# A routed FFN whose expert pairs add the shared rows and scatter the finished rows into the output

## The chip, the cores and the metric

The kernel runs on one core of one Trainium2 chip. The metric is the device time of one execution in microseconds (us). The kernel before has a median of 659.03 us over three runs (658.07 to 661.3).

## The reference

Four sequences of 1024 tokens with 128 features go through an attention-like recurrence and then through a mixture-of-experts FFN. Only these parts matter here:

```python
# attention: of the 3*N outputs (two of each three zero) the last N are kept
z = jnp.zeros_like(o)
out = jnp.stack([z, z, o], axis=2).reshape(B, 3 * N, H, HD)[:, -N:]
...
x = x + attention(layernorm(x))
# FFN on layernorm(x): one expert of 16 for each token, and a shared FFN for all
_, top_idx = jax.lax.top_k(logits, 1)
scores = jax.nn.sigmoid(logits) * mask
masked_inputs = scores.T[:, :, None] * x[None, :, :]
gate_up = jnp.einsum('eth,ehf->etf', masked_inputs, gate_up_proj)
gate, up = jnp.split(gate_up, 2, axis=-1)
expert_out = jnp.einsum('etf,efh->eth', up * jax.nn.silu(gate), down_proj)
shared = jax.nn.silu(x @ w_gate.T) * (x @ w_up.T) @ w_down.T
out = x + shared + expert_out.sum(axis=0)
```

Since only every third attention output row is not zero, only every third token (1368 in all, "mixed") depends on the recurrence. The other 2728 ("others") can go through the FFN early.

## The kernel before

Token rows lie in the SBUF tile `xf` as 33 rows of 128 features in each of 128 partitions: row `3*s` (eleven of them) holds mixed tokens, the remaining 22 hold others. Some places at the sequences' ends hold no token.

The routed part of either set runs as follows. A routing step on VectorE gives every row a slot in a table in memory in which the rows of one expert lie in whole tiles of 128 (`idx`). POOL scatters the normed and scaled rows by indirect DMA, one tile of 128 rows each, into `xs_others` or `xs_mixed` (`scatter`, line 1010). Two tiles make a pair. For each pair, SP loads the rows (`load`, line 510), TensorE transposes them (line 1895), multiplies by the expert's gate and up weights (line 1901), transposes the hidden rows (1908) and multiplies by the down weights (1918). ScalarE applies silu (887) and copies between PSUM and SBUF (881 for the rows, 891 for the hidden, 896 for the output in `copy_y`), VectorE multiplies gate by up (1345). SP stores the pair's output `e_y` into `ys_...` (line 517). Rows, silu results and outputs are double-buffered by the pair's parity. The order of each engine's work in a pair is written out by hand: TensorE does the first gate projection of pair k+1, the hidden transposes of k, the second gate projection of k+1, the row transposes of k+2, the down projection of k. `over_pairs` runs the pairs in a hardware loop, two per turn, with the last three or four written out behind it.

Others have 38 tiles: twelve pairs run beside the recurrence's chain, seven within its forward steps. Mixed rows have 26 tiles, thirteen pairs (`RUNS[2]`), which run alone at the end of the kernel. Before them stand, in this order, the end of the attention, the norm and the routing of the mixed rows, their scatter (line 1010, eleven DMAs on POOL) beside the shared FFN of the mixed rows (lines 1837, 1838, 846, 1331, 1847; line 1336 adds it to `xf`), and VectorE's add of the others' expert rows to `xf` (line 1618), after which `s_fin` reaches 1.

After the last pair, POOL waits for all stores and gathers the outputs back by slot into `early` (line 1026, eleven DMAs). VectorE adds them to `xf` in two halves (line 1629). SP, once `s_fin` is 1, issues the stores of the other rows to `out` (lines 663 to 667), then those of the mixed rows of each half (line 672); ScalarE issues the rows at the sequences' ends (990, 991). All waits stand in program order on their engine's queue: SP's stores of the other rows stand behind all thirteen pairs. The tables are filled with zeros early on (lines 595, 597), so that unused slots hold zeros. TensorE has two clock levels, and the profile shows the granted share (1.00 or 0.50).

Of the kernel before, what the change touches and what calls it, by code (L numbers as in the profile page):

```python
# [6 lines left out]
F32 = mybir.dt.float32  # L7
# [58 lines left out]

def constants():
# [13 lines left out]
    for t in (OTHERS, MIXED):  # L81
        v = valid[:, t.rows]
        parts["valid_" + t.name] = v
        spare = np.where(v, 0, t.tiles * P + np.cumsum(~v.ravel()).reshape(v.shape) - 1)
        parts["spare_" + t.name] = spare
        assert (~v).sum() <= P
    parts["prefer"] = np.tile(E - np.arange(E)[None, :], (P, 1))
# [100 lines left out]
def build(nc, a, out, xs, ys, scr):  # L188

    ctx = ExitStack()  # L190
    with ctx:
# [7 lines left out]
        normed = nc.dram_tensor("normed", (B, N, D), F32).ap()  # L199

# [4 lines left out]
        eps = sb("eps", [P, 1])  # L205
        warm = sb("warm", [P, 3])
# [107 lines left out]
        for t in (MIXED, OTHERS):  # L314
# [12 lines left out]
            else:  # L327
                rows, scaled = take(t.n * D), take(t.n * D)
                q["rows"] = q["shared"] = [rows[:, j * D:(j + 1) * D] for j in range(t.n)]
                q["scaled"] = [scaled[:, j * D:(j + 1) * D] for j in range(t.n)]  # L330
                q["back"] = rows
# [23 lines left out]
        def xT_shared(t, g):  # L355
# [9 lines left out]
        assert 4 * U * P <= left.shape[1]  # L365
        e_in, e_xT = (left[:, k * 2 * U * P:(k + 1) * 2 * U * P].rearrange("p (b u d) -> p b u d", b=2, u=U)
                      for k in (0, 1))
# [40 lines left out]
        s_gat, s_fin, s_out = {t: two("s_gathered_" + t) for t in fb}, sem("s_final"), sem("s_out")  # L408
        s_ends = sem("s_out_ends")
# [3 lines left out]
        PARTS = ((0, MIXED.n // 2 + 1), (MIXED.n // 2 + 1, MIXED.n))  # L413
# [55 lines left out]
        def over_pairs(engine, run, pair):  # L469
# [3 lines left out]
            looped = (n - 3) // 2 * 2  # L473
            with engine.Fori(0, looped // 2) as half:
                i = half * 2
                for k in (0, 1):
                    pair(i, k, 3)
# [17 lines left out]

        def middle_rows(b):

            n = 3 * SKIP
            return out[b, ROWS - n:(C - 1) * ROWS - n:3, :].rearrange("(g r) d -> g r d", r=L2)
# [25 lines left out]
        def _(sp):  # L525
# [68 lines left out]
            for t in SETS:  # L594
                sp.dma_start(xs[t.name].rearrange("(m p) d -> p m d", p=P),
                             zeros[:, 0:D].unsqueeze(1).to_broadcast([P, t.tiles + 1, D])).then_inc(s_xz, 16)
                sp.dma_start(ys[t.name][t.tiles * P:, :], zeros[:, 0:D]).then_inc(s_xz, 16)
# [63 lines left out]
            for b in range(B):  # L661
                g0 = b * C
                sp.dma_start(out[b:b + 1, 1:ROWS - n, :], xf[g0:g0 + 1, n + 1:, :]).then_inc(s_out, 16)
                for q in (1, 2):
                    sp.dma_start(out[b, ROWS - n + q:(C - 1) * ROWS - n:3, :].rearrange("(g r) d -> g r d", r=L2),
                                 xf[g0 + 1:g0 + C - 1, q::3, :]).then_inc(s_out, 16)
                    sp.dma_start(out[b:b + 1, N - last + q:N:3, :],
                                 xf[g0 + C - 1:g0 + C, q:last:3, :]).then_inc(s_out, 16)
            for part, (lo, hi) in enumerate(PARTS):
                sp.wait_ge(s_fin, 2 + part)  # L670
                for b in range(B):
                    sp.dma_start(middle_rows(b)[:, lo:hi, :], xf[b * C + 1:b * C + C - 1, 3 * lo:3 * hi - 2:3, :]
                                 ).then_inc(s_out, 16)
            sp.wait_ge(s_out, 16 * 7 * B)
            sp.wait_ge(s_ends, 16 * 2 * B)
        @block.scalar
        def _(act):
# [220 lines left out]
            def pairs(run):  # L898
                def pair(i, k, ahead):
# [7 lines left out]
                    copy_y(run, i, k, k % 2, i * 8 + 16 * (k // 2 + 1 + run.base[k % 2]))  # L907
# [77 lines left out]
            n = 3 * SKIP  # L985
            last = N - ((C - 1) * ROWS - n)
            act.wait_ge(s_fin, 3)
            for b in range(B):
                g0 = b * C
                act.dma_start(out[b:b + 1, 0:1, :], xf[g0:g0 + 1, n:n + 1, :]).then_inc(s_ends, 16)  # L990
                act.dma_start(out[b:b + 1, N - last:N:3, :], xf[g0 + C - 1:g0 + C, 0:last:3, :]).then_inc(s_ends, 16)
# [6 lines left out]
        def _(pool):  # L998
            G.memset(zeros[:], 0.0).then_inc(s_zero, 1)
            G.memset(eps[:], LN_EPS).then_inc(s_zero, 1)  # L1000
            G.memset(xf[:], 0.0).then_inc(s_xfz, 1)
            pool.wait_ge(s_wa, 128)
# [4 lines left out]
            def scatter_tile(t, j):  # L1007
                q = fb[t.name]
                pool.wait_ge(s_sc, TB[t.name] + j + 1)
                G.indirect_dma_start(xs[t.name], bass.IndirectOffsetOnAxis(ap=q["idx"][:, j:j + 1].bitcast(U32), axis=0),  # L1010
                                     q["scaled"][j], None).then_inc(s_scat[t.name], 16)
# [8 lines left out]
            def gather(t, pairs):  # L1020
# [4 lines left out]
                for j in range(t.n):  # L1025
                    G.indirect_dma_start(q["back"][:, j * D:(j + 1) * D], None, ys[t.name],  # L1026
                                         bass.IndirectOffsetOnAxis(ap=q["idx"][:, j:j + 1].bitcast(U32), axis=0)
                                         ).then_inc(s_gat[t.name][int(t is MIXED and j >= PARTS[1][0])], 16)
# [130 lines left out]
            pool.wait_ge(s_fa, GA[MIXED.name] + len(MIXED.groups))  # L1159
            m = RUNS[2].n  # L1160
# [905 lines left out]
```

## Time and profile before

| what | us |
|---|---|
| median of three runs | 659.03 |
| profiled execution | 659.8 |
| its span, first to last instruction | 657.7 |
| TensorE matmul busy | 518.7 (79%) |
| VectorE busy | 488.9 (74%) |
| POOL busy | 363.0 (55%) |
| ScalarE busy | 255.3 (39%) |
| mean granted TensorE clock | 0.934 |

The profiled execution took 2.1 us more than its span. Busy shares are averages over stages with different limits. The chain of work that ended last is made of 35% TensorE, 28% VectorE, 14% issue time, 12% POOL and 5% DMA; the mixed pairs and what follows them are its last 81 us. In the rows, "start us, us" are the start and the duration, and "issue" is time in which an engine waited for nothing that the profile shows.

### The profile page before, as it was taken

The page shows a single profiled execution, that of the slowest core. Times are in us where ns is not written, and L with a number is a line of the kernel's source. Part 1 is how long each engine was busy: PE and PEld are TensorE (multiplying, and loading weights), DVE is VectorE, ACT ScalarE, POOL GpSimd, SP SyncE. Part 2 cuts the span into 40 slices and gives each one's busy share as a digit, 9 for nine tenths or more (in the row PEclk, how much of TensorE's full clock was granted, in tenths as well). Part 3 has the DMA queues.
Part 4 walks back from the last instruction along what each step waited for, and adds up shares of the span by engine and source line. Part 5 has one row for each costly group of instructions (what it writes and reads, how often), then busy time and mean ns, then how long its engine had stood idle before and what let it go on. Part 6 is the DMA issues. An engine that isn't in the chain of part 4 may idle for free.

```text
span 657.7 us, 7388 instructions
## 1 busy us (share of the span) xinstructions
PE 518.7 (79%) x1809; PEld 268.9 (41%) x1810; DVE 488.9 (74%) x787; ACT 255.3 (39%) x538; POOL 363.0 (55%) x352
## 2 busy tenths in 40 slices
PE   1778989999999888766878689889999967488930
PEld 0434444445454434222355355434553254245520
DVE  3559999989898999899899998588999766312201
ACT  1815744344535342111433245525545014044510
POOL 4335767666667675565688344476667575600033
PEclk9968999999999998899999799999999977889985
DMA  9601115900000484000431123100100021122134
GB/s 224 140 0 32 33 40 131 258 0 1 0 1 0 119 283 142 1 0 0 118 95 37 40 77 99 49 16 24 32 16 17 5 53 36 43 61 64 56 83 113
DMA packets 46754, 41.79 MB, mean 64 GB/s; under 512 B 4636, under 2 KB 40296, under 8 KB 46216
## 3 DMA queue, kind: packets, MB, share of 16 engines
q1 hardware_dynamic: 43140, 35.61, 19.8%
q0 software_dynamic: 2448, 5.38, 2.9%
q10 hardware_dynamic: 1136, 0.46, 0.3%
q8 instruction: 12, 0.20, 0.1%
q14 instruction: 18, 0.15, 0.1%
HBM read 23.80 MB, written 17.63 MB: 63 GB/s over the span
## 4 chain that ended last, share of the span: by engine, by line
PE 35%; DVE 28%; issue 14%; POOL 12%; DMA 5%; ACT 2%; ACTq 1%; POOLq 0%; DVEq 0%; SPq 0%
DVE grown L1447 9%; PE ps L1901 9%; PE ps L1918 5%; DVE ps L1486 4%; POOL grown L1079 4%; PE ps L1858 4%; PE ps L1908 2%; DVE early L1551 2%; PE ps L1859 2%; DVE grown L1474 2%; PE ps L1958 2%; POOL uv L995 2%; POOL early L1026 2%; PE ps L1663 2%; PE ps L1959 2%
## 5 line engine op out<-in xcount | busy, mean ns | idle before, releaser
L1079 POOL TENSOR_TENSOR grown<-grown 128x512 f32<-128x512 f32 x64 | 80.5, 1266 | 101.0 <-DVE grown L1474 100.8
L1447 DVE TENSOR_TENSOR grown<-ps,steps 128x1536 f32<-128x1536 f32 x64 | 112.1, 1752 | 1.8
L1858 PE MATMUL ps<-grown,cst 128*128 128x512 f32 x128 | 76.3, 680 | 29.4 <-DVE grown L1447 29.3
L870 ACT ACTIVATE uv<-ps 128x512 f32<-128x512 f32 x64 | 38.1, 597 | 109.3 <-DVE grown L1474 109.3
L1901 PE MATMUL ps<-steps 128*128 x128 | 68.7, 635 | 8.5 <-issue 8.5
L1859 PE MATMUL ps<-grown,cst 128*128 128x512 f32 x128 | 69.7, 628 | 0.0
L995 POOL TENSOR_TENSOR uv<-uv,steps 128x512 f32<-128x512 f32 x64 | 67.5, 1075 | 1.6 <-ACT uv L870 1.6
L1345 DVE TENSOR_TENSOR e_h<-rk,ps 128x256 f32<-128x256 f32 x64 | 25.4, 417 | 53.1 <-ACT rk L887 34.3
L1866 PE MATMUL ps<-uv,cst 128*128 128x512 f32 x128 | 60.4, 594 | 0.6 <-POOL uv L995 0.6
L1152 POOL TENSOR_TENSOR early<-state,qT 128x512 f32 x22 | 37.2, 1689 | 34.0 <-DVE state L1461 34.0
L1474 DVE TENSOR_TENSOR grown<-ps,steps 128x512 f32<-128x512 f32 x64 | 43.3, 677 | 8.7 <-PE ps L1858 8.5
L1858 PEld LDWEIGHTS ps<-grown,cst 128*128 128x128 f32 x128 | 22.1, 204 | 63.2 <-DVE grown L1447 57.2
L1486 DVE TENSOR_TENSOR ps<-ps,grown 128x512 f32<-128x512 f32 x60 | 41.6, 693 | 8.3 <-POOL grown L1079 8.3
L1026 POOL DMA_INDIRECT early<-ys_mixed,slots_mixed x11 | 10.6, 964 | 64.5 <-DMA ys_mixed<-e_y 61.5
L1480 DVE TENSOR_TENSOR ps<-ps,steps 128x512 f32<-128x512 f32 x64 | 44.1, 689 | 1.8 <-PE ps L1859 1.8
L1123 POOL COPY early<-early 128x32 f32<-128x32 f32 x63 | 27.3, 435 | 27.9 <-DVE early L1556 27.8
L1551 DVE TENSOR_TENSOR early<-early 128x256 f32<-128x256 f32 x63 | 40.2, 638 | 1.3
L1859 PEld LDWEIGHTS ps<-grown,cst 128*128 128x128 f32 x128 | 26.2, 205 | 34.5 <-issue 34.5
L887 ACT ACTIVATE rk<-ps 128x256 f32<-128x256 f32 x64 | 23.9, 383 | 40.1 <-PE ps L1901 38.4
L1918 PE MATMUL ps<-steps,e_hT 128*128 x256 | 35.8, 283 | 2.7 <-ACT e_hT L891 2.7
L1866 PEld LDWEIGHTS ps<-uv,cst 128*128 128x128 f32 x128 | 24.2, 190 | 31.8 <-issue 29.7
L1918 PEld LDWEIGHTS ps<-steps,e_hT 128*128 128x128 f32 x256 | 31.5, 191 | 8.9 <-issue 8.0
(223 smaller groups left out, 998.5 us busy)
## 6 DMA issues: line engine op xcount, KB each, us to landing
steps<-gate_up_proj SPq DMA_DIRECT2D x1, 4096.0 KB, 16.9
xs_others<-zeros SPq DMA_DIRECT2D x1, 2496.0 KB, 10.9
steps<-xs_others SPq DMA_DIRECT2D x19, 128.0 KB, 2.2
ys_others<-e_y SPq DMA_DIRECT2D x19, 128.0 KB, 1.8
early<-chain_m SPq DMA_DIRECT2D x4, 512.0 KB, 6.1
xf<-x SPq DMA_DIRECT2D x4, 495.0 KB
normed<-early SPq DMA_DIRECT2D x28, 64.0 KB, 1.7
xs_mixed<-zeros SPq DMA_DIRECT2D x1, 1728.0 KB, 9.0
```

The costliest lines, as they stand in the source:

```text
L995: return G.tensor_tensor(wide(dst, w), wide(src, w), per_col(tile, k, 1, h, w), ALU.mult)
L1079: G.tensor_tensor(decayed[:, h], decayed[:, h], work[:, h, 1], ALU.add).then_inc(s_add[h], 1)
L1447: V.tensor_tensor(grown[:, :, h].rearrange("p e (x w) -> p e x w", w=HD), st, per_col(tile, FF, 3, h, HD), ALU.mult).then_inc(s_prod[h], 1)
L1474: V.tensor_tensor(wide(work[:, h, 1], HD), wide(ps[h][:, 1], HD), per_col(tile_of(i), PP, 1, h, HD), ALU.mult).then_inc(s_uterm[h], 1)
L1480: V.tensor_tensor(wide(bank[2 * h], HD), wide(bank[2 * h], HD), per_col(tile_of(i), K, 1, h, HD), ALU.mult).then_inc(s_term[h], 1)
L1486: V.tensor_tensor(dst, bank[2 * h], decayed[:, h], ALU.add).then_inc(s_state[h], 1)
L1551: V.tensor_tensor(ch_pr[:, m % 2, :, :, 0:HD], ch_m[r][:, :, i, :].rearrange("p j i -> p i j").unsqueeze(1) .to_broadcast([P, 4, HD, HD]), ...
L1858: T.matmul(bank[2 * h + 1], c["block"], work[:, h, 1], start=True, stop=True).then_inc(s_usum[h], 1)
L1859: T.matmul(bank[2 * h], c["minus"], work[:, h, 0], start=True, stop=True).then_inc(s_red[h], 1)
L1866: T.matmul(bank[4 + h], c["ident"], vterm[:, h], start=i in (0, L1), stop=i + 1 in (L1, NT)).then_inc(s_ba[h], 1)
L1901: T.matmul(b_gu(run, b)[u], e_xT[:, b, u], gu[:, bass.ds(ex * (2 * F), 2 * F)], start=True, stop=True).then_inc(s_eg, 1)
L1918: ins = T.matmul(b_y(run)[:, u * D:(u + 1) * D], e_hT[:, u, f * P:(f + 1) * P], dw[:, bass.ds(ex[u] * F + f * D, D)], start=(f == 0), stop ...
```

## The change

It touches the mixed rows alone.

- Each normed row goes to its slot with a 129th number behind it, the row of `out` to which its token belongs (`token_mixed`, written by one ScalarE instruction). The table `slot_rows` is filled early with zero rows whose number is 4096, one past the last row of `out`.
- After the slot scatter POOL scatters the eleven tiles of base rows (`xf`: input, attention and shared FFN) by the same slots into `ys_mixed`, which is now zeroed whole.
- In the pairs SP loads rows with their numbers, and later the pair's base rows (`e_base`). POOL copies the row numbers to whole numbers (`e_to`). VectorE adds the base to the output in PSUM (`add_base`) instead of ScalarE's copy. POOL scatters both tiles of the pair straight into `out`, leaving out rows numbered 4096.
- The gather, the final adds and the stores of the mixed rows go. SP issues the stores of the other rows between the loads, two per pair from the third pair on.
- In the mixed run the first two pairs are written out ahead of the loop on all engines; POOL and SP have all thirteen written out.

The diff, cut to its core:

```diff
+def tokens_of(t):
+    tok = 3 * L2 * (np.arange(P)[:, None] % C) - 3 * SKIP + np.asarray(t.rows)[None, :]
+    return np.where((tok >= 0) & (tok < N), N * (np.arange(P)[:, None] // C) + tok, 0)
...
+            alone = 2 if run.t is MIXED else 0
+            looped = alone + (n - 3 - alone) // 2 * 2
+            for k in range(alone):
+                pair(0, k, n - 1 - k)
+            with engine.Fori(alone // 2, looped // 2) as half:
...
# SP, early: fills
+            sp.wait_ge(s_none, 2)
+            sp.dma_start(slots.rearrange("(m p) d -> p m d", p=P),
+                         no_row[:].unsqueeze(1).to_broadcast([P, MIXED.tiles + 1, D + 1])).then_inc(s_xz, 16)
+            sp.dma_start(ys[MIXED.name].rearrange("(m p) d -> p m d", p=P),
+                         zeros[:, 0:D].unsqueeze(1).to_broadcast([P, MIXED.tiles + 1, D])).then_inc(s_xz, 16)
...
# SP, mixed pairs
-            pairs_in_out(sp, RUNS[2])
+            def load_rows(k):
+                sp.wait_ge(s_et, k + run.g0 - 1 if k >= 2 else run.g0)
+                if k >= 2:
+                    sp.wait_ge(s_to, k - 1)
+                sp.dma_start(e_row[:, k % 2], x_in[:, k * U:(k + 1) * U, :]).then_inc(s_ei[k % 2], 16)
+            def load_base(k):
+                sp.wait_ge(s_eo, k + run.g0)
+                sp.dma_start(e_base[:, k % 2], base_in[:, k * U:(k + 1) * U, :]).then_inc(s_eb[k % 2], 16)
...
+            stores = [(b, part) for b in range(B) for part in range(5)]
+            for k in range(3):
+                load_rows(k)
+            sp.wait_ge(s_based, 16 * MIXED.n)
+            for k in range(2):
+                load_base(k)
             sp.wait_ge(s_fin, 1)
+            for k in range(2, run.n):
+                if k + 1 < run.n:
+                    load_rows(k + 1)
+                load_base(k)
+                for b, part in stores[2 * k - 4:2 * k - 2]:
+                    store_others(b, part)
+            sp.wait_ge(s_out, 16 * 5 * B)
+            for k in (0, 1):
+                sp.wait_ge(s_sent[k], 16 * U * ((run.n + 1 - k) // 2))
...
# ScalarE
-                    copy_y(run, i, k, k % 2, i * 8 + 16 * (k // 2 + 1 + run.base[k % 2]))
+                    if run.t is OTHERS:
+                        copy_y(run, i, k, k % 2, i * 8 + 16 * (k // 2 + 1 + run.base[k % 2]))
...
+            S.activation(q["token"], c["token_mixed"], ACT.Copy).then_inc(s_sc, 1)
...
# POOL, after scatter(MIXED)
-            pool.wait_ge(s_fa, GA[MIXED.name] + len(MIXED.groups))
-            m = RUNS[2].n
-            gather(MIXED, (RUNS[2].base[0] + (m + 1) // 2, RUNS[2].base[1] + m // 2))
+            for g, (lo, hi) in enumerate(MIXED.groups):
+                pool.wait_ge(s_fa, GA[MIXED.name] + g + 1)
+                for j in range(lo, hi):
+                    G.indirect_dma_start(ys[MIXED.name],
+                                         bass.IndirectOffsetOnAxis(ap=q["idx"][:, j:j + 1].bitcast(U32), axis=0),
+                                         xf[:, MIXED.rows[j]], None).then_inc(s_based, 16)
+            def tokens(k):
+                pool.wait_ge(s_et, k + run.g0 + 1)
+                G.tensor_copy(e_to[:, k], e_row[:, k % 2, :, D]).then_inc(s_to, 1)
+            for k in (0, 1):
+                tokens(k)
+            for k in range(run.n):
+                if k + 2 < run.n:
+                    tokens(k + 2)
+                pool.wait_ge(s_to, k + 1)
+                pool.wait_ge(s_eo, k + run.g0 + 2)
+                for u in range(U):
+                    G.indirect_dma_start(out_rows, bass.IndirectOffsetOnAxis(ap=e_to[:, k, u:u + 1].bitcast(U32), axis=0),
+                                         e_y[:, k % 2, u], None, bounds_check=B * N - 1, oob_is_err=False
+                                         ).then_inc(s_sent[k % 2], 16)
...
# VectorE
+            def add_base(i, k):
+                run, b = RUNS[2], k % 2
+                dve.wait_ge(s_ey, i + (k + run.g0 + 1))
+                dve.wait_ge(s_eb[b], i * 8 + 16 * (k // 2 + 1))
+                if type(i) is not int or i + k >= 2:
+                    dve.wait_ge(s_sent[b], i * (8 * U) + 16 * U * (k // 2))
+                else:
+                    dve.wait_ge(s_ew[b], 16 * (1 + run.base[b]))
+                V.tensor_tensor(e_y[:, b], b_y(run).rearrange("p (u d) -> p u d", u=U), e_base[:, b], ALU.add
+                                ).then_inc(s_eo, 1)
             def pair(i, k, ahead):
                 if ahead:
                     gate(RUNS[2], i, k + 1, (k + 1) % 2)
+                add_base(i, k)
```

## Rows read from the trace of the kernel before

**Rows 1.** Chain that ended last, from 630 us on: start us, us, what.
```profile
630.11 1.17 PE ps L1918 x8
...
631.70 1.80 DMA ys_mixed<-e_y
...
634.30 0.99 POOL early L1026
...
647.00 3.04 DMA early<-ys_mixed,slots_mixed
...
650.06 0.83 DVE xf L1629
```

**Rows 2.** Timeline after the last pair, DMA issues of SP and ScalarE: start us, us.
```profile
632.49 1.01 SPq L665 DMA_DIRECT2D out<-xf  x1
...
655.21 0.78 ACTq L991 DMA_DIRECT2D out<-xf  x1
```

**Rows 3.** Chain that ended last, the first mixed pairs.
```profile
576.35 0.68 PE ps L1895 x2
...
582.53 0.88 PE ps L1901 x2
583.41 0.22 PE ps L1895 x2
...
588.37 0.80 issue
589.17 1.12 PE ps L1901 x2
...
592.78 0.17 issue
```

**Rows 4.** The page's costliest groups (busy, mean ns) and DMA issues (KB, us to landing).
```profile
L1345 DVE TENSOR_TENSOR e_h<-rk,ps 128x256 f32<-128x256 f32 x64 | 25.4, 417 | 53.1 <-ACT rk L887 34.3
...
steps<-xs_mixed SPq DMA_DIRECT2D x13, 128.0 KB, 2.2
```

**Rows 5.** Timeline of POOL beside the chain, and where the mixed slots are ready.
```profile
324.39 0.25 POOL L1123 COPY early<-early 128x32 f32<-128x32 f32 x1
...
555.95 0.17 DVE L1315 TENSOR_TENSOR slots_mixed<-early,cst 128x11 int32<-128x11 f32 x1
...
556.93 1.00 POOL L1010 DMA_INDIRECT xs_mixed<-early,slots_mixed  x1 [6.06 <-issue]
```

**Rows 6.** Lines 1010 and 1026: ns min/median/max, first and last start; then line 1010's landing.
```profile
L1010 POOL DMA_INDIRECT xs_mixed<-early,slots_mixed x11: 963/967/3156, 556.9 to 569.7; - x11
...
DMA to landing us min/median/max: 2.2/2.2/4.4
...
L1026 POOL DMA_INDIRECT early<-ys_others,slots_others x22: 947/952/1079, 523.3 to 549.9; - x22
```

**Rows 7.** Timeline at the last slot scatter: VectorE and POOL.
```profile
568.91 3.08 DVE L1618 TENSOR_TENSOR xf<-xf,early 128x2816 f32<-128x2816 f32 x1
569.68 3.16 POOL L1010 DMA_INDIRECT xs_mixed<-early,slots_mixed  x1 [0.30 <-issue]
```

**Rows 8.** Stretches of 2 us: busy by engine, granted clock (PEclk), DMA share, GB/s.
```profile
568.00:570.00 2.00, 0.41 (x4) 0.21 (x2) 1.56 (x2) 0.00 (x0) 1.39 (x3) 1.00 0.14 47
570.00:572.00 2.00, 0.00 (x0) 0.00 (x0) 2.00 (x1) 0.00 (x0) 2.00 (x1) 0.60 0.06 18
...
580.00:582.00 2.00, 2.00 (x6) 0.71 (x5) 0.80 (x2) 0.68 (x2) 0.00 (x0) 0.84 0.01 2
```

**Rows 9.** Timeline in pair 0: weight loads of the gate projection.
```profile
578.82 0.33 PEld L1901 LDWEIGHTS ps<-steps 128*128 128x128 f32 x1 [0.52 <-issue]
579.67 0.33 PEld L1901 LDWEIGHTS ps<-steps 128*128 128x128 f32 x1 [0.52 <-issue]
```

**Rows 10.** Timeline of SP's queue around the early fills.
```profile
122.12 5.00 SPq L597 DMA_DIRECT2D ys_mixed<-zeros  x1
220.05 0.38 SPq L613 DMA_DIRECT2D chain_m<-state  x1
```

More of the change, by code:

```diff
@@ L86, in constants @@
         assert (~v).sum() <= P
+    parts["token_mixed"] = tokens_of(MIXED)
     parts["prefer"] = np.tile(E - np.arange(E)[None, :], (P, 1))
@@ L199, in build @@
         normed = nc.dram_tensor("normed", (B, N, D), F32).ap()
+        slots = nc.dram_tensor("slot_rows", ((MIXED.tiles + 1) * P, D + 1), F32).ap()
+        out_rows = out.rearrange("b n d -> (b n) d")
         cst = sb("cst", [P, CONST.shape[1]])
@@ L327, in build @@
             else:
-                rows, scaled = take(t.n * D), take(t.n * D)
+                rows, scaled = take(t.n * D), take(t.n * (D + 1))
                 q["rows"] = q["shared"] = [rows[:, j * D:(j + 1) * D] for j in range(t.n)]
-                q["scaled"] = [scaled[:, j * D:(j + 1) * D] for j in range(t.n)]
-                q["back"] = rows
+                q["sent"] = [scaled[:, j * (D + 1):(j + 1) * (D + 1)] for j in range(t.n)]
+                q["scaled"] = [r[:, 0:D] for r in q["sent"]]
+                q["token"] = scaled.rearrange("p (n d) -> p n d", d=D + 1)[:, :, D]
                 q["lg"] = take(t.n * E)
@@ L407, in build @@
                                                 sem("s_e_out"), two("s_e_written"))
-        s_gat, s_fin, s_out = {t: two("s_gathered_" + t) for t in fb}, sem("s_final"), sem("s_out")
-        s_ends = sem("s_out_ends")
+        s_gat, s_fin, s_out = sem("s_gathered"), sem("s_final"), sem("s_out")
+        s_to, s_sent, s_none = sem("s_e_tokens"), two("s_e_sent"), sem("s_no_row")
+        s_based, s_eb = sem("s_bases_scattered"), two("s_e_base")
         SETS = (OTHERS, MIXED)
@@ L656, in _ @@
             sp.wait_ge(s_scat[MIXED.name], 16 * MIXED.n)
-            pairs_in_out(sp, RUNS[2])
+            x_in = slots.rearrange("(m p) d -> p m d", p=P)
+            base_in = ys[MIXED.name].rearrange("(m p) d -> p m d", p=P)
+            run = RUNS[2]
+            def load_rows(k):
[3 more added lines that the diff above has]
+                sp.dma_start(e_row[:, k % 2], x_in[:, k * U:(k + 1) * U, :]).then_inc(s_ei[k % 2], 16)
@@ L669, in _, with store_others @@
[L669 to L675, printed above, removed]
+            def store_others(b, part):
+                g0 = b * C
+                if part == 0:
+                    sp.dma_start(out[b:b + 1, 1:ROWS - n, :], xf[g0:g0 + 1, n + 1:, :]).then_inc(s_out, 16)
+                elif part < 3:
+                    sp.dma_start(out[b, ROWS - n + part:(C - 1) * ROWS - n:3, :].rearrange("(g r) d -> g r d", r=L2),
+                                 xf[g0 + 1:g0 + C - 1, part::3, :]).then_inc(s_out, 16)
+                else:
+                    sp.dma_start(out[b:b + 1, N - last + part - 2:N:3, :],
+                                 xf[g0 + C - 1:g0 + C, part - 2:last:3, :]).then_inc(s_out, 16)
@@ L983, in _ @@
             pairs(RUNS[2])
[L985 to L991, printed above, removed]
         def pool_tt(dst, src, tile, k, h, w):
@@ L1624, in pair @@
                     gate(RUNS[2], i, k + 1, (k + 1) % 2)
+                add_base(i, k)
             over_pairs(dve, RUNS[2], pair)
-            for part, (lo, hi) in enumerate(PARTS):
-                dve.wait_ge(s_gat[MIXED.name][part], 16 * (hi - lo))
-                V.tensor_tensor(rows_of(xf, MIXED, lo, hi), rows_of(xf, MIXED, lo, hi),
-                                tiles_of(fb[MIXED.name]["back"][:, lo * D:hi * D], MIXED), ALU.add).then_inc(s_fin, 1)
         @block.tensor
```

50 lines of the change are left out of this document (23 added, 27 removed).

## The prediction

> **What bounds the kernel now.** I read the chain that ended last from its end backwards, then the timeline of the DMA queues beside it, then the chain one stage earlier. The chain's tail [rows 1] begins with TensorE's last down projection, which starts at 630.11 and ends near 631.27. After it come ScalarE's copy, a 1.80 us store of the pair from 631.70 on, 0.8 us until POOL starts, eleven gathers whose starts go from 634.30 to 647.00 (12.70/10 = 1.27 us each), 3.04 us until the last has landed and a 0.83 us add, which ends at 650.89. Behind it ScalarE issues the last of eight small stores at 655.21 for 0.78 us [rows 2], and the span ends at 657.7. So 657.7 - 631.3 = 26.4 us pass after the last expert matmul, with no TensorE work. Before that the thirteen mixed pairs run at TensorE's pace: from one pair's start at 589.17 to the next at 592.78 + 0.17 = 592.95 it is 3.78 us, and 4.4 us (0.80 instead of 0.17 of issue time) where the loop turns over [rows 3]. The bound of this stage is therefore TensorE, and that of the tail is a serial string of POOL issues and DMA landings.
>
> **What is removed and what replaces it.** Gone are the gather of eleven tiles, the two halves of the final add, the stores of the mixed rows and ScalarE's copy of each pair's output. In their place VectorE adds a loaded base to the PSUM output of every pair, and POOL scatters the pair's two tiles into the output. Only the last pair's part stays behind the last matmul. Terms: the add has 256 columns with one operand in PSUM, like the gate's 128x256 multiply at 0.417 us [rows 4], say 0.45 with its wait. POOL's wake is priced by the other indirect DMA that waited on a semaphore: VectorE's slot instruction started at 555.95 and took 0.17, POOL started at 556.93, so 0.81 us [rows 5]. Second scatter one step of 1.27 after the first; landing 2.2 us from its start is the median of the scatters, 3.04 that of the last gather [rows 6, 1], and I take 2.5, nearer to the scatters. Sum 0.45 + 0.81 + 1.27 + 2.5 = 5.0, with 0.1 for the last wait 5.1 us. Gain in the tail: 26.4 - 5.1 = 21.3 us, or 20.7 with the longer landing.
>
> **What the change adds ahead of the pairs.** Here it costs. The base rows go through memory too: eleven more scatters stand on POOL's queue behind the eleven of the normed rows, ahead of the copies of the row numbers. The next loads wait for these copies. POOL's last normed-row scatter starts at 569.68 and takes 3.16 us instead of 0.967, because VectorE's 3.08 us add over xf (568.91 to 571.99) is running: its end plus one ordinary scatter gives 572.84 [rows 7, 6]. So base scatter 1 starts at 572.84 + 0.30 = 573.1, the eleventh ten steps of 1.27 later at 585.8, and it is done at 586.8. The shared FFN's groups on which they wait are finished by 568.9 (the xf add of [rows 7] is queued behind them), so that wait is nothing. The first copy of row numbers takes no more than the 0.25 us POOL copy between two scatters [rows 5], until 587.1. SP has been held at the third load of rows by exactly this copy; it issues at 587.3 and such a load lands in 2.2 us [rows 4]: 589.5. TensorE wants these rows in the middle of pair 0, ahead of that pair's down projection: before, their two transposes stood at 583.41 and took 0.22 us of the chain [rows 3]. TensorE now waits until 589.55, 6.1 us. The first base is not later than that: the eleventh base scatter lands at 588.0, two loads follow, 590.4, while pair 0's down projection ends at about 591.
>
> That wait has a second price, TensorE's clock. TensorE's last matmul of the shared part ends at 568.4 (0.41 us of work in 568 to 570). The granted clock averages 0.60 between 570 and 572 and 0.50 afterwards, which is the lower of the two levels (1.2 GHz); TensorE starts again at 576.35 [rows 3], and the average of 0.84 in 580 to 582 puts its rise to 2.4 GHz at 580.6, 4.3 us after the restart [rows 8]. The new wait of 6.1 us is nearly as long as that idle time (7.9 us), of which the first 2.0 us passed at the higher level, so I expect the same. At the lower level the weight loads of the gate projection stand 0.86 us apart (578.82, 579.67) [rows 9], against 0.88 us for two such matmuls at the higher one (582.53) [rows 3]: twice the time. In 4.3 us fit the two transposes (0.68 us at 576.35 instead of 0.22, +0.46), a down projection (about 1 us at the higher level; +0.7, an estimate between nothing and double) and the first gate projection (+0.86): 2.0 us lost, bounds 0 (no fall) and 2.3.
>
> The two first pairs are now written out ahead of the loop on all engines: one loop turn fewer, -(0.80 - 0.17) = -0.6 us [rows 3]. Start side in all: 6.1 + 2.0 - 0.6 = +7.5 us.
>
> **Within the pairs.** VectorE gets 0.42 more for every pair and has two gates of 0.42 there, 1.3 us of 3.78. The add can hold back the next down projection only if the base is late (it is asked for two pairs ahead) or its buffer's scatter isn't home. From one add, 0.81 + 1.27 + 2.2 to 3.0 = 4.3 to 5.1 us bring the pair's scatter home, and the buffer is needed again after 7.56 - 0.45 = 7.1 us: covered. POOL needs 2 x 1.27 + 0.25 + 0.15 = 2.9 us a pair, 3.5 with a wake: covered in 3.78, by 0.3 us only. SP's queue is the thin spot: the load of the rows for pair k+2 now stands behind the wait for add k-2 and two stores of the other rows, a large one of which holds SP for 1.01 us [rows 2]. It issues 0.5 + 0.4 + 1.8 = 2.7 us after the start of pair k-1, lands 2.2 us later at 4.9, and the rows are wanted at 3.78 + 2.4 = 6.2: 1.3 us of cover. Should stores and scatters lengthen a landing by that much, each further us is TensorE's; bounds 0 and 8 x 1.0 us, and I take 0.8 us in all. The ScalarE copy that goes frees an engine that was not late.
>
> **Early parts.** Zeroing the mixed outputs grows from 64 KB to 1.7 MB. The last zero store now leaves SP's hand at 127.1, and SP's next DMA is at 220.05 [rows 10]; another 8 to 10 us there are hidden by over 90 us. The filling of the empty row stands on POOL ahead of its wait for the weights. The copy of the row numbers on ScalarE (about 0.2 us) ends long before the slots at 556.1. All three at nothing.
>
> **Sum.** End 657.7 - 21.3 + 7.5 + 0.8 = 644.7 us of span. The profiled run took 659.8, 2.1 us over its span, and stands 0.8 above the median of 659.03. So 644.7 + 2.1 - 0.8 = 646.0 us, 13 us or 2.0% faster.
>
> **Rivals.**
> (a) *The clock stays up and the loads keep their cover*: 646.0 - 2.0 - 0.8 = 643.2. For it: the wait is nearly 2 us shorter than the one before. Against: the fall in [rows 8] comes 2.0 us after the last matmul.
> (b) *SP's queue becomes the bound of the pairs*: cover of 1.3 us is gone, some 1 us on eight pairs, 646 + 7 = 653. For it: rows, bases and stores share one queue in a fixed order. Against: the stores at the end were issued without a pause, and the gathers beside them started every 1.27 us all the same [rows 1, 2].
> (c) *The scatter with a limit is dearer, and POOL becomes the bound*; this is the one that ends slower. No instruction of the trace skips rows over a bound. Its price is bounded below by 0.95 us, the plain form [rows 6]. With x for one, POOL needs 2(x + 0.3) + 0.4 a pair, which reaches 3.78 at x = 1.4. From there every tenth of a us costs 0.2 us on each of eleven pairs, 2.2 us. At x = 1.95, about double, it is 12 us: 658, no change; above 2.15 it is slower, and 2.4 gives 668. Nothing in the trace speaks for a double price except the lack of a row.
> (d) *The long scatter of [rows 7] was no collision but a queue that had filled up.* Then the eleven scatters right behind it would cost 3.16 each, and TensorE would wait 10 x 2.2 us more: 668. Against: twenty-two gathers in a row had a maximum of 1.079 us [rows 6], and the long scatter ends 0.85 us after VectorE's add does, about one scatter's own time. By the Trainium skill, page SBUF — State Buffer, section Who interferes with whom, `tensor_tensor` was not seen to stall DMAs of this queue (a reason is inferred there), which would favour (d); the same section lets a VectorE instruction with two SBUF inputs block a GpSimd one that reads SBUF, and an indirect DMA does read its row numbers there. I side with the row.
> (e) *No gain because the end is set elsewhere*, by SP's stores: they are all issued by pair 11, so only if (b) is extreme; part of (b).
>
> **Chances.** Forecast 0.56; (a) 0.14; (b) 0.16; (c) 0.09, half of it slower, the rest about the same; (d) 0.03; something unnamed at the start of the pairs, 0.02. Range: from 641, which is (a) with 2.2 us off for an earlier landing or add, to 656, which is (b) with the longest landing. Outside lie most of (c) and (d). A measurement of this kernel can tell about 0.5%, 3.3 us: below 655.7 faster, 0.87; within, 0.06; above 662.3 slower, 0.07.
>
> **What would show it.** In the changed profile: a POOL row of eleven base scatters up to about 587; an idle time of TensorE of some 6 us ahead of a transpose in pair 0, released by a load of rows; the granted clock at 0.5 for about 4 us from 589; pairs 3.8 us apart afterwards; POOL rows of about 1 us for the bounded scatter; about 5 us between the last matmul and the end. Wrong would be a pair distance over 4.2 us, scatters over 1.4 us, or adds that wait for scatters to land.

## The result and the profile after

| | before | after |
|---|---|---|
| median of four runs, us | 660.16 (658.07 to 662.94) | 653.95 (652.99 to 655.9) |
| ratio, 95% interval | | 0.9871 [0.9836, 0.9905] |
| profiled execution, us | 659.8 | 654.4 |
| its span, us | 657.7 | 652.4 |
| mean granted TensorE clock | 0.934 | 0.934 |

The change makes the kernel 1.3% faster, 6.2 us, where 13 us were forecast. The reading below asks where the other part went, 7.7 us of span (652.4 instead of 644.7).

The chain that ended last, around the slot scatters and pair 0 (start us, us, what):

```profile
570.76 0.97 POOL slot_rows L1048
571.72 0.30 issue
572.03 3.17 POOL slot_rows L1048
575.20 0.30 issue
575.51 0.97 POOL ys_mixed L1202
...
588.23 0.97 POOL ys_mixed L1202
589.20 0.21 POOL e_to L1210
589.47 2.13 DMA steps<-slot_rows
591.61 0.04 issue
591.65 0.69 PE ps L1965 x2
592.34 1.72 PE ps L1988 x8
594.06 1.71 PE ps L1971 x2
```

The last slot scatter starts at 572.03 (before: 569.68, [rows 7]) and again takes 3.17 us beside VectorE's 3.08 us add. Then come the eleven base scatters, the copies of the row numbers, the third load and TensorE's transposes, in the order that the prediction gave. The timeline shows how long TensorE waited there (in brackets), and TensorE's clock is in the table of stretches (busy by engine in the order of [rows 8], granted clock, DMA share, GB/s):

```profile
571.28 3.08 DVE L1679 TENSOR_TENSOR xf<-xf,early 128x2816 f32<-128x2816 f32 x1
...
591.65 0.69 PE L1965 MATMUL ps<-cst,steps 128*128 128x128 f32 x2 [5.30 <-DMA steps<-slot_rows]
```

```profile
590.00:592.00 2.00, 0.35 (x2) 0.30 (x3) 0.00 (x0) 0.00 (x0) 0.00 (x0) 0.65 0.44 119
592.00:594.00 2.00, 2.00 (x11) 2.00 (x10) 0.00 (x0) 0.39 (x1) 0.19 (x1) 0.50 0.53 144
594.00:596.00 2.00, 2.00 (x6) 0.86 (x5) 0.42 (x1) 0.19 (x1) 0.58 (x1) 0.50 0.15 46
596.00:598.00 2.00, 2.00 (x7) 1.19 (x7) 0.42 (x1) 0.81 (x3) 1.41 (x2) 0.64 0.53 123
598.00:600.00 2.00, 1.90 (x12) 1.30 (x11) 0.85 (x2) 0.64 (x2) 0.19 (x1) 1.00 0.34 98
```

TensorE idles 5.30 us and then works 5.8 us at the lower level (1.2 GHz): the 0.64 of 596 to 598 puts the rise at 597.4. Its first down projection takes 1.72 us; that of the same pair took 0.95 in the chain of the kernel before (at 583.63).

The end of the timeline:

```profile
641.12 1.15 PE L1988 MATMUL ps<-steps,e_hT 128*128 x8 [0.89 <-ACT e_hT L933]
642.31 0.42 DVE L1692 TENSOR_TENSOR e_y<-ps,uv 128x256 f32<-128x256 f32 x1 [2.06 <-PE ps L1988]
642.39 0.98 POOL L1220 DMA_INDIRECT out<-e_y,e_to  x1 [0.30 <-issue]
643.68 0.98 POOL L1220 DMA_INDIRECT out<-e_y,e_to  x1 [0.30 <-issue]
644.97 0.98 POOL L1220 DMA_INDIRECT out<-e_y,e_to  x1 [0.30 <-issue]
```

The last matmul ends at 642.27, the last scatter's instruction at 645.95. But the span ends at 652.4. What fills the rest is no work on data. It is found under the line of the program's end block, where each engine's queue closes with an instruction named DRAIN (duration ns min/median/max, first and last start). First the changed kernel, then the one before:

```profile
L198 POOLq DRAIN  x1: 8260/8260/8260, 643.9 to 643.9; - x1
L198 SPq COMPARE_BRANCH  x1: 38/38/38, 647.1 to 647.1; - x1
...
L198 POOLq EVENT_SEMAPHORE  x2: 17/17/17, 652.2 to 652.3; - x2
```

```profile
L191 POOLq DRAIN  x1: 14992/14992/14992, 638.8 to 638.8; - x1
...
L191 SPq COMPARE_BRANCH  x1: 38/38/38, 657.3 to 657.3; - x1
```

After: SP has seen the last scatter land at 647.1, and everybody waits for POOL's DRAIN until 643.9 + 8.26 = 652.16. Before: POOL's DRAIN ended at 638.8 + 14.99 = 653.8, hidden behind the stores for which SP waited until 657.3. The change took that long tail away, and with it the cover of the DRAIN, whose last 5.0 us now stand bare at the end (652.16 - 647.1). Nobody had priced them.

### The profile page after: what moved, and what is told of

Its sections match the earlier page's. It is cut to its first block, busy times and chain, and to the rows that moved or that the text cites. A ratio compares the mean times of both kernels' runs of the same rounds, so it can differ in the third digit from the quotient of the medians.

```text
span 652.4 us, 7380 instructions
## 1 busy us (share of the span) xinstructions
PE 525.5 (81%) x1809; PEld 273.8 (42%) x1810; DVE 492.3 (75%) x798; ACT 250.6 (38%) x526; POOL 392.1 (60%) x393
## 4 chain that ended last, share of the span: by engine, by line
PE 35%; DVE 28%; issue 15%; POOL 13%; DMA 4%; ACT 2%; ACTq 1%; POOLq 0%; DVEq 0%; SPq 0%
DVE grown L1508 10%; PE ps L1971 9%; PE ps L1988 5%; POOL grown L1118 4%; DVE ps L1547 4%; PE ps L1928 3%; PE ps L1978 2%; POOL slot_rows L1048 2%; PE ps L2028 2%; POOL uv L1031 2%; PE ps L1929 2%; DVE grown L1535 2%; DVE early L1612 2%; POOL ys_mixed L1202 2%; DVE grown L1501 2%
## 5 line engine op out<-in xcount | busy, mean ns | idle before, releaser
L1928 PE MATMUL ps<-grown,cst 128*128 128x512 f32 x128 | 76.8, 684 | 28.2 <-DVE grown L1508 28.0
L1971 PE MATMUL ps<-steps 128*128 x128 | 70.6, 650 | 8.6 <-issue 8.2
L1929 PE MATMUL ps<-grown,cst 128*128 128x512 f32 x128 | 70.7, 636 | 0.0
L1220 POOL DMA_INDIRECT out<-e_y,e_to x26 | 25.6, 984 | 25.2 <-DVE e_y L1692 20.9
```

Of the source, the lines that this page charges most:

```text
L1928: T.matmul(bank[2 * h + 1], c["block"], work[:, h, 1], start=True, stop=True).then_inc(s_usum[h], 1)
L1929: T.matmul(bank[2 * h], c["minus"], work[:, h, 0], start=True, stop=True).then_inc(s_red[h], 1)
L1971: T.matmul(b_gu(run, b)[u], e_xT[:, b, u], gu[:, bass.ds(ex * (2 * F), 2 * F)], start=True, stop=True).then_inc(s_eg, 1)
```

## The experiments

The kernel before took 663.8 us on the two chips of e1 to e8 and 675.9 on the two of e9 to e12, so kernels are compared by their ratio to it and by stretches of a profile. The changed kernel itself was not run again on these chips. e2, e5, e6 and e7 are single runs, and only their profiles are used. Four numbers are read from each profile. Two are stretches: from a named event to the end of the last matmul, and from that to the end. The third is the "lag": the end of POOL's last DRAIN minus the end of its last DMA instruction. (`G.drain()` in the code puts one more such DRAIN on POOL's queue.) The fourth is the number of POOL DMAs since the last drain (97 in the changed kernel: 49 up to the last gather of the others' rows, then 11 + 11 + 26 scatters).

**e1: the last two pairs stored by SP.** They go in slot order into `ys_mixed`, so their rows are missing from `out`. Does POOL's part after the last matmul set the end?

```diff
-            for k in range(run.n):
+            for k in range(run.n - 2):      # POOL's scatters into out
...
+            for k in range(run.n - 2, run.n):   # SP
+                sp.wait_ge(s_eo, k + run.g0 + 2)
+                sp.dma_start(base_in[:, k * U:(k + 1) * U, :], e_y[:, k % 2]).then_inc(s_out, 16)
```

> The changed kernel, but the outputs of the last two pairs are not scattered by POOL: SP stores them in slot order into the table ys_mixed (so these rows of the output are left out). Theory A (the 5 us behind the last landing are POOL's DRAIN, which ends about 6.1 us after POOL's last indirect DMA, whatever else happens): POOL's last scatter is then that of pair 10, about 4 us before TensorE's last matmul, its drain is over about when SP's last store lands, and the end comes 3 us behind TensorE's last matmul instead of 10.1; span about 645.5 against 652.4, with the stretches before unchanged. Rival B (a fixed ending of some 5 us behind the last DMA landing, whoever issued it): TensorE's last matmul + 0.5 + 2 + 5 = 7.5 us, span about 650.

645.77 us, ratio 0.9726 [0.965, 0.9801]; the end comes 3.4 us behind the last matmul (643.08 to 646.5) instead of 10.1. SP sees its last store land at 645.7. POOL's last DMA ends at 640.41 and its DRAIN ends 5.9 us later:

```profile
L198 POOLq DRAIN  x1: 7843/7843/7843, 638.5 to 638.5; - x1
```

So what follows the last matmul on POOL sets the end, and even here the DRAIN ends last, by 0.6 us. It is no fixed ending behind the last landing either: that was 5.3 us (652.4 - 647.1) and is 0.8 us here.

**e2: POOL waits for its own scatters first.** If the DRAIN waits for transfers to land, it is short once they have landed; if it is work of its own, it starts later and the end moves little.

```diff
+            for k in (0, 1):     # POOL, behind its last scatter
+                pool.wait_ge(s_sent[k], 16 * U * ((run.n + 1 - k) // 2))
```

> The changed kernel, but POOL itself waits until all its scatters have landed before its part of the program ends. Theory A1 (the drain costs some 6 us from where it starts): it then starts after the landing instead of beside it, and the end moves from 5.3 us to 6.1 us or more behind the last landing, +1 to +2 us. Theory A2 (the drain only waits for something that the last indirect DMA set off, done about 6.1 us after that DMA's end): the end stays where it is, 6.2 us behind POOL's last DMA. Rival B (fixed ending behind the landing): also unchanged, but then e1 shows 5 us behind SP's store.

653.01 us in one run, span 651.0.

```profile
L198 POOLq COMPARE_BRANCH  x1: 38/38/38, 644.4 to 644.4; - x1
L198 SPq COMPARE_BRANCH  x1: 37/37/37, 644.4 to 644.4; - x1
L198 POOLq DRAIN  x1: 6197/6197/6197, 644.6 to 644.6; - x1
```

POOL knows at 644.4 that all has landed, starts its DRAIN at 644.6, and the DRAIN lasts 6.2 us all the same. It isn't waiting for data. It also starts later in relation to the last DMA, whose end is 643.25, and lags 7.5 us instead of 6.2. The end comes 11.4 us behind the last matmul instead of 10.1.

**e3: no base scatters.** The base is left out of the output; pairs load zeros in its place. It prices the start side as a whole.

```diff
-                    G.indirect_dma_start(ys[MIXED.name], ..., xf[:, MIXED.rows[j]], None).then_inc(s_based, 16)
-            sp.wait_ge(s_based, 16 * MIXED.n)
+            sp.wait_ge(s_xz, 64)
```

> The changed kernel without the eleven scatters of the base rows and without SP's wait for them (the base that is added is then zero, so these rows of the output lack it). Theory A (they hold back the copy of the row numbers on POOL, that holds back SP's third load, and TensorE waits in pair 0): the wait of 5.3 us ahead of the transposes of pair 0 is gone, TensorE's clock stays up from pair 0 on (another 2 us), and the time from the last slot scatter's start to the last expert matmul falls from 70.2 to about 62.5 us; total about 7.5 us shorter. Rival (the loads themselves are late because rows, bases and stores share SP's queue): the wait in pair 0 stays above 2 us.

645.46 us, ratio 0.9721 [0.9656, 0.9786]. From the last slot scatter's start to the last matmul's end it takes 62.6 us (569.92 to 632.53), against 70.2 after and 61.6 before. The eleven base scatters cost 7.6 us, clock included (7.1 against e2, where this part is as in the changed kernel and takes 69.7 us).

**e4: one scatter for both parts.** The whole result again. The slot table gets 257 numbers a row (normed row, row number, base); the shared FFN's sum is written there instead of into `xf`; POOL scatters once; VectorE's 3.08 us add waits until the scatters have landed.

```diff
-        slots = nc.dram_tensor("slot_rows", ((MIXED.tiles + 1) * P, D + 1), F32).ap()
+        slots = nc.dram_tensor("slot_rows", ((MIXED.tiles + 1) * P, 2 * D + 1), F32).ap()
...
+                dst = fb[t.name]["base"][:, lo:hi] if t is MIXED else rows_of(xf, t, lo, hi)
+                V.tensor_tensor(dst, rows_of(xf, t, lo, hi), ..., ALU.add).then_inc(s_fa, 1)
...
+            dve.wait_ge(s_scat[MIXED.name], 16 * MIXED.n)   # ahead of the add of the others
```

> A version meant to be faster, with the full output: normed row, row number and base row of 257 numbers go to the slot in one scatter, each group of tiles as soon as the shared FFN's add of its group is done, and VectorE's big add over xf is put behind the landing of these scatters. POOL issues eleven DMAs instead of twenty-two. Theory: the last slot scatter starts about 574.5 (after the add of the third group at 571.4 and three steps of 1.27 us) and takes 1 us instead of 3.17, so the pairs start when they do now, within 1 us, but TensorE no longer waits in pair 0 and keeps its clock: 7 us less than the changed kernel, about 0.976 of the kernel before. Rival (rows of 1028 bytes make scatters or landings longer, or loads of parts of such rows are slower): POOL rows over 1.1 us or landings over 3 us, and less than 4 us of gain.

645.92 us (644.64 to 648.48), ratio 0.9741 [0.9689, 0.9792], span 642.9. The last slot scatter and the moved add:

```profile
572.75 0.97 POOL L1048 DMA_INDIRECT slot_rows<-early,slots_mixed  x1 [0.30 <-issue]
...
575.36 3.09 DVE L1676 TENSOR_TENSOR xf<-xf,early 128x2816 f32<-128x2816 f32 x1 [5.45 <-DMA slot_rows<-early,slots_mixed]
```

With the add out of its way the last scatter takes 0.97 us instead of 3.17, though it writes twice the bytes; and the wait of pair 0 is gone. With 86 POOL DMAs the lag is 5.3 us. The interval of the ratio lies clear below that of the changed kernel (0.9836 to 0.9905).

**e5: a drain where POOL is idle.** The changed kernel with one `G.drain()` on POOL ahead of the slot scatter, where it waits over 6 us for VectorE. If a DRAIN costs by the DMAs since the last one, the one at the end gets cheaper.

```diff
             gather(OTHERS, RUNS[2].base)
+            G.drain()
             scatter(MIXED)
```

> The changed kernel with one more DRAIN on POOL, between the gather of the others and the mixed slot scatter, where POOL idles for 7.4 us. POOL has issued 49 of its 97 DMAs by then. Theory S (the drain settles every DMA that POOL has issued since the last one, one after another: 6.2 us / 97 = 64 ns each, as in e2; e3 and e4 with 86 DMAs show 5.4): the drain in the idle time takes about 3.1 us, the one at the end has 48 DMAs left and also takes 3.1 us, so the end comes about 3 us earlier against TensorE's last matmul (7 us behind it, from 10.1). Theory F (code for the drain is loaded at its first use): the first takes about 6 us, the second under 1 us beyond the last landing, so the end is 5 us behind the last matmul. Theory W (a fixed 6 us at every drain): both take 6.2 us and the end stays at 10 us.

650.32 us in one run, span 648.2. The drain in the middle lags 4.1 us behind its last gather and is hidden. The one at the end lags 4.0 instead of 6.2 (3.1 were expected), and the end comes 7.9 us behind the last matmul instead of 10.1. Had the cost been one of first use, the second DRAIN would have been all but free. So the DRAIN at the end has a cost that grows with the number of POOL DMAs since the last drain (48 left here).

**e6: TensorE kept busy in the wait of pair 0.** The changed kernel with five matmuls that nobody reads in that wait.

```diff
+                    if run.t is MIXED and type(i) is int and i + k == 0:
+                        for _ in range(5):
+                            T.matmul(bank[3], c["ident"], work_all[:, 0:4 * P], start=True, stop=True)
```

> The changed kernel; while TensorE waits in pair 0 for the third load of rows, it runs five more matmuls of 128x512 into a bank that nobody reads (0.86 us each, 4.3 us of the 5.3 us wait). Theory (the wait costs the clock as well): the granted clock stays at 1.00 through pairs 0 and 1, the down projection of pair 0 takes 0.97 instead of 1.72 us and the time from the transposes after the wait to the last matmul of the mixed pairs falls by about 2 us, from 50.6 to about 48.6. Rival (the clock falls whatever TensorE does, or the pairs after the wait are bound by loads): 50.6 stays.

651.69 us in one run. TensorE's idle time ahead of the transposes is 1.49 us, and the granted clock stays at 1.00:

```profile
590.00:592.00 2.00, 1.13 (x9) 1.01 (x10) 0.00 (x0) 0.38 (x1) 0.19 (x1) 1.00 0.65 184
592.00:594.00 2.00, 1.71 (x10) 0.99 (x9) 0.42 (x1) 0.20 (x1) 0.30 (x1) 1.00 0.28 78
```

From these transposes to the last matmul's end it takes 48.68 us instead of 50.62. The same stretch is 50.1 to 50.5 in e1, e2 and e5, which have the same wait, so the low clock cost 1.4 to 1.9 us; the prediction had 2.0.

**e7: no stores between the loads.** The stores of the other rows are left out; the pairs' loads stand alone on SP's queue. This tests rival (b).

```diff
-                for b, part in stores[2 * k - 4:2 * k - 2]:
-                    store_others(b, part)
```

> The changed kernel without the twenty stores of the other rows between the loads (these rows of the output are left out). Theory (TensorE's pairs are bound by TensorE, SP's queue and the DMA engines have cover): pair starts as far apart as now, 3.8 to 4.4 us, the whole stretch of pairs within 0.5 us, and TensorE waits in pair 0 just as long. Rival (the stores lengthen the loads of rows): the stretch from pair 2 to pair 12 gets shorter by 1 us or more.

651.85 us in one run. The stretch of e6 is 49.96 us here, against 50.62 after and 50.1 to 50.5 in e1, e2 and e5. The stores cost the pairs 0.7 us at the most. Rival (b) is out.

**e8: e4 and e5 together.** The whole result.

> The version of e4 (one scatter for row, number and base) with the additional DRAIN of e5. By theory S the last drain has 37 of 86 DMAs left, 2.4 us instead of 5.4, partly beside the landing: 2.5 to 3 us less than e4, about 643 us, 0.970 of the kernel before. By F the last drain is all but gone: 4.2 us less than e4. By W no gain over e4.

643.44 us (638.21 to 644.63), ratio 0.9709 [0.966, 0.9759], span 639.5. The end comes 7.0 us behind the last matmul (e4: 9.9), and the lag is 3.1 us with 37 DMAs left. The ratios' intervals of e4 and e8 overlap, so the step between them is shown by the lag and not by the total.

**e9: e8 with five matmuls ahead of the pairs.** TensorE waits 8.3 us there for the first rows, and the clock falls, before the change too [rows 8].

```diff
             pe.wait_ge(s_idx, 2)
+            for _ in range(5):
+                T.matmul(bank[3], c["ident"], work_all[:, 0:4 * P], start=True, stop=True)
             pairs(RUNS[2])
```

> The kernel of e8 (one scatter per pair, drain of GpSimd ahead of the mixed slot scatter) with five more 128x512 matmuls into a bank that nobody reads, placed in TensorE's 8.3 us wait ahead of the first mixed pair. Nothing is left out. In e8 the first transposes of the pairs start at 576.90 and the last matmul ends at 632.47, 55.6 us, with the granted clock down until about 582. If the low clock there costs 1.7 to 2.0 us, as e6 showed for the changed kernel, this stretch is 53.6 to 53.9 us and the time is 641.5 us (ratio to before about 0.968). Rival: the clock falls anyway, or what TensorE gains there is waited for at the next transfer: 55.6 us and 643.4 us.

658.97 us, ratio 0.9738 [0.9705, 0.9771]. From the first transposes to the last matmul's end 55.25 us, against 55.57 in e8: a miss. The five end 3.16 us before the rows come, and the clock falls all the same, only later:

```profile
592.00:594.00 2.00, 0.00 (x0) 0.00 (x0) 1.54 (x1) 0.00 (x0) 0.00 (x0) 1.00 0.23 56
594.00:596.00 2.00, 0.75 (x4) 0.54 (x5) 1.55 (x1) 0.38 (x1) 0.34 (x1) 0.90 0.81 207
596.00:598.00 2.00, 2.00 (x5) 0.97 (x4) 0.00 (x0) 0.39 (x1) 0.19 (x1) 0.50 0.38 75
```

**e10: e9 with drains in pair 0 and ahead of the tenth pair's scatters.**

```diff
             for k in (0, 1):
                 tokens(k)
+            G.drain()
             for k in range(run.n):
+                if k == 9:
+                    G.drain()
```

> The kernel of e9 with two more drains of GpSimd, both where GpSimd has nothing to do: behind the first two mixed groups of token indices in its wait for pair 0, and before the scatter of the tenth pair. Nothing is left out. Theory S (a drain costs by the number of GpSimd transfers since the last one): some 8 transfers are left for the drain at the end instead of 37, so it ends 1.2 to 1.5 us behind GpSimd's last transfer instead of 3.1, and the time is 1.5 to 2 us below e9, 639.5 to 640. Rival: the drain at the end has a fixed part of 3 us (no gain), or the drains in the middle delay a scatter or a load that TensorE waits for (0 to 2 us slower than e9).

659.78 us, ratio 0.975 [0.9718, 0.9782]: no gain over e9. Eight DMAs are left and the last lag is 1.5 us, as expected. But the second of the new drains stands in the way:

```profile
640.45 0.98 POOL L1219 DMA_INDIRECT out<-e_y,e_to  x1 [0.30 <-issue]
...
644.38 0.19 POOL L1206 CAST e_to<-steps 128x2 int32<-128x2 f32 x1 [2.95 <-issue]
```

POOL stands still for 2.95 us, the next scatters come late, and TensorE has 2.24 us of idle time ahead of its last down projection (e9: 0.89). After it the clock falls once more, and that down projection takes 1.81 us instead of 1.15:

```profile
650.00:652.00 2.00, 0.04 (x1) 0.05 (x1) 0.00 (x0) 0.60 (x1) 1.22 (x3) 1.00 0.01 0
652.00:654.00 2.00, 1.76 (x8) 1.47 (x8) 0.00 (x0) 0.00 (x0) 0.88 (x1) 0.57 0.05 9
```

The stretch from the first transposes to the last matmul's end grows from 55.25 to 57.18, 1.93 us: 1.35 more of idle time and 0.66 by the clock make 2.0. What was won at the end (1.6 us of lag) was lost there: the rival came true. The new drain in pair 0 took 1.2 us and delayed nothing.

**e11: e8 once more**, as the yardstick of e12.

> The kernel of e8 once more, unchanged, as the yardstick for e12 on one and the same chip, since e9 and e10 ran on a chip on which the kernel before takes 676 us and which shows waits of 13 us at instruction issue around 530 us. Nothing is left out. Both theories: ratio to before 0.966 to 0.976, 55.6 us from the first transposes of the mixed pairs to the end of the last matmul, GpSimd's last drain ending 3.1 us behind its last transfer.

659.86 us (655.51 to 661.9), ratio 0.9755 [0.9712, 0.9799]; stretch 55.16 us, lag 3.1.

**e12: eight matmuls, and of the two new drains only that of pair 0.**

```diff
             for k in (0, 1):     # on top of e8
                 tokens(k)
+            G.drain()
...
+            for _ in range(8):
+                T.matmul(bank[3], c["ident"], work_all[:, 0:4 * P], start=True, stop=True)
             pairs(RUNS[2])
```

> The kernel of e8 with eight more 128x512 matmuls that nobody reads in TensorE's 8.3 us wait ahead of the pairs (e9 had five, which left 3.2 us idle, and the clock fell all the same), and of the two further drains of e10 only the one in GpSimd's wait for pair 0, which took 1.2 us there and delayed nothing. Nothing is left out. At the 0.91 us of one in e9 the eight fill 7.3 us and leave some 1 us idle. If a short idle time is what keeps the clock up (e6: 1.5 us idle, clock 1.00), 53.6 to 53.9 us from the first transposes to the end of the last matmul instead of 55.6; 26 transfers are left for the last drain, which by the line through e5 and e8 ends 2.1 to 2.3 us behind GpSimd's last transfer instead of 3.1. Together 2.5 to 3 us below e11. Rival for the clock: it falls in pair 0 whatever fills the wait: 55.6 us; then only the drain's 0.8 to 1 us is left. Rival for the eight matmuls: they last longer than the wait and start the pairs late, by up to 1 us.

655.57 us (653.12 to 658.62), ratio 0.9709 [0.9666, 0.9752]. TensorE idles 0.44 us ahead of the first transposes, and the clock stays up:

```profile
586.28 7.13 PE L2103 MATMUL ps<-grown,cst 128*128 128x512 f32 x16 [1.13 <-issue]
593.85 0.42 PE L1964 MATMUL ps<-cst,steps 128*128 128x128 f32 x2 [0.44 <-DMA steps<-slot_rows]
```

```profile
594.00:596.00 2.00, 1.53 (x7) 0.80 (x7) 0.81 (x1) 0.77 (x2) 0.69 (x2) 1.00 0.46 131
596.00:598.00 2.00, 2.00 (x8) 0.90 (x7) 0.84 (x2) 0.93 (x3) 0.00 (x0) 1.00 0.52 130
```

The stretch is 53.66 us, 1.5 below e11, and the lag is 2.2 us with 26 DMAs left, 0.9 below e11. These 2.4 us are what the two edits did. The medians differ by 4.3; the profiled run of e11 reached its first transposes 4.0 us later than that of e12, in code that both share and behind unexplained waits (last section), so the rest is not put down to the edits. The ratios' intervals overlap, so that the step from e8 to e12 is shown by the stretches, not by the total.

## Why the prediction was right in sign and twice too large

Point by point, in spans of the profiled executions (forecast 644.7, measured 652.4, +7.7):

| term | forecast | measured |
|---|---|---|
| end behind the last matmul | 5.1 | 10.1 (642.27 to 652.4) |
| last slot scatter's start to last matmul's end, change | +8.3 (7.5 + 0.8) | +8.65 (61.6 to 70.2) |
| everything ahead of that scatter | 0 | +2.35 (569.68 to 572.03) |

*The tail is the step that failed.* Its sum (0.45 + 0.81 + 1.27 + 2.5, and 0.1) ends at the landing of the last scatter, and that was right: 647.1 - 642.27 = 4.8 us. What the sum left out is POOL's DRAIN behind it, +5.0 us. The prediction read the tail of the kernel before as a chain of gathers, add and stores; the DRAIN was hidden there, since it ended 3.5 us before SP had seen the stores land. One row of that chain did name its line, in the place of a gather, and the prediction passed over it:

```profile
639.07 1.26 POOLq L191
```

To cost what is left when a cover goes, all that ends in that stretch has to be listed, the queues' own instructions too. e1, e2 and e5 show the mechanism.

The number of POOL DMAs since the last drain, and the lag:

| kernel | e10 | e12 | e8, e9, e11 | e5 | e4 | e1 | after |
|---|---|---|---|---|---|---|---|
| DMAs | 8 | 26 | 37 | 48 | 86 | 93 | 97 |
| lag, us | 1.5 | 2.2 | 3.1 | 4.0 | 5.3 | 5.9 | 6.2 |

From 26 to 97 DMAs it grows by 4.0 us, 0.056 us each on average. The steps are uneven: 0.9 us for eleven slot or base scatters (e12 to e8, e4 to after), 2.2 us for the 49 early DMAs (e5 to after, e8 to e4). Number is not all: the drain of the kernel before lags 5.85 us with 71 DMAs, and the one ahead of e10's tenth pair 2.9 us with 18. Both stand right behind transfers that carried rows, while the last pairs' scatters write nothing on this data (POOL's queue moved 0.00 MB after 640 us in the changed kernel). Whether that makes the difference, and what the DRAIN does in its time, was not settled.

*The start side was right.* The string of eleven scatters at 1.27 us, the 3.17 us one, the third load, the wait (5.30 in the timeline, forecast 6.1), the clock (1.4 to 1.9 by e6, forecast 2.0, though it stayed low for 5.8 us and not 4.3) and pairs mostly 3.8 to 4.6 us apart: together +8.65 against +8.3, and e3 gives 7.6 for the base scatters alone.

*The part ahead of it is probably not the change's.* e2 and e3 have the same work up to there and start that scatter at 569.9; e7 at 570.1, e5 at 570.5, e6 at 571.2, e1 at 573.1. The 2.35 us lie within this spread of 3.2 us between executions. All of them start later than the 569.68 of the one profile before, so that a part of it comes from the change isn't excluded. The forecast had no term for it, though it set one profiled run against another.

*Rivals.* (a) The clock did not stay up. (b) e7 left 0.7 us of it at the most. (c) The scatter with a limit takes 980/982/1004 ns (min/median/max of 26), the price of the plain one; the slower case never came near. (d) The eleven scatters behind the long one took 0.963 to 0.968 us each, and e4 shows what made it long: with VectorE's add moved away it takes 0.97. The Trainium skill (SBUF — State Buffer, section Who interferes with whom) saw no stall of this queue's DMAs by `tensor_tensor`; here the measurement decides, 3.17 us beside the add and 0.97 without it, for a DMA that reads its row numbers from SBUF. It agrees with another rule of the same section of the Trainium skill, that a VectorE instruction with two SBUF inputs contends with a GpSimd instruction that reads SBUF. (e) named the end being set elsewhere, but looked only at SP's stores. It was the right question at the wrong queue.

The measured 653.95 lies near the upper end of the range (641 to 656), which rival (b) had set. Rival (b) did not come about, and the cause that took the time there was in none of the cases. That the time lies within the range is luck.

## What to carry to other kernels

When a change takes away work at the end, list everything that ends in the last stretch of the old kernel, the end block's DRAIN of every queue among it, and ask what each will cost without its cover. This kernel pays for its DMAs on GpSimd once more in the last drain. A drain put where GpSimd waits anyway takes a part of that away (2.2 us off the lag in e5, and in e8 against e4), but one put where GpSimd has little to spare gives it back (e10). And two scatters of the same slots were better made one wider scatter (e4's span is 9.5 us shorter than that of the changed kernel), with large VectorE instructions kept away from it.

## What the runs showed of the hardware that was not expected

- The GpSimd DRAIN at the end lasts on when all its transfers have landed: 6.2 us after 97 DMAs in e2.
- Beside VectorE's 3.08 us add of two SBUF tiles the scatter that ran with it took 3.14 to 3.17 us in all eight kernels that had the two side by side (before, after, e1 to e3, e5 to e7), and 0.97 in e4.
- A scatter of 257 numbers a row costs POOL the same 0.97 us as one of 129 (e4).
- TensorE's clock stayed at 1.00 over idle times of 1.49 us (e6) and 0.44 us (e12) and fell after 2.24 us (the end of e10), 3.16 us (e9) and 5.30 us (after).
- On the chips of e9 to e12 the stretch from 530 us on has waits that the other two don't show. ScalarE's row of e9, and the same instruction in e8:

```profile
542.85 0.30 ACT L741 ACTIVATE rstd_mixed<-mv_mixed,eps 128x11 f32<-128x11 f32 x1 [13.37 <-remote]
```

```profile
534.72 0.30 ACT L741 ACTIVATE rstd_mixed<-mv_mixed,eps 128x11 f32<-128x11 f32 x1 [7.82 <-DVE mv_mixed L1242]
```

The first profile attributes 13.37 us to nothing on the core, and the last slot scatter starts at 589.8 instead of 572.0. The kernel before is 12 us slower there too (675.99 and 675.79 against 663.8). The cause stays open.
